# GPS graph layer: edge sums kept as 512 columns and a degree in a buffer of 750 nodes and projected once per chunk, with seven ring buffers in place of six

## The reference, cut to what matters

```python
# N = 6250 nodes of D = 256 columns, E = 106250 edges sorted by dst
xn = layernorm(x)
m = xn[src] @ W[:256] + edge_attr @ W[256:]              # one row for each edge
deg = segment_sum(ones, dst, 6250)
norm = where(deg > 0, rsqrt(max(deg, 1)), 0)
h = segment_sum(m * norm[dst][:, None], dst, 6250) + h_bias
x = x + h + mix(xn)      # mix: linear attention over all nodes, 8 heads, then a GELU MLP
x = x + ffn(layernorm(x))  # two of eight experts, chosen by the mean of all rows, then a layernorm
```

## Time and profile before

| | us |
|---|---|
| median of 3 runs | 1607.79 (1602.73 to 1609.69) |
| the profiled execution, its own time | 1606.56 |
| its span, first to last instruction | 1604.4 |
| busy in the span: PE / PEld / DVE / ACT / POOL | 1129.4 / 741.1 / 671.4 / 543.1 / 918.7 |
| moved by DMA | 294.98 MB, mean 184 GB/s |
| mean granted TensorE clock | 0.877 of full |

### The profile page before, as it was taken

One profiled execution on the slowest core, in us unless ns is written; L12 is line 12 of the kernel. 1 busy time (PEld: TensorE's weight loads), 2 busy tenths in 40 slices (PEclk: granted clock), 3 DMA queues, 4 the chain that ended last, 5 costly groups with the idle time before them and its releaser, 6 DMA issues.

```text
span 1604.4 us, 22019 instructions
## 1 busy us (share of the span) xinstructions
PE 1129.4 (70%) x6879; PEld 741.1 (46%) x6879; DVE 671.4 (42%) x1784; ACT 543.1 (34%) x1129; POOL 918.7 (57%) x974
## 2 busy tenths in 40 slices
PE   0166757665676775565677777776777749999997
PEld 0023323332332332233344344444444449999997
DVE  5633334343433443321323233233332446677675
ACT  4731111111111111101233333333333356767673
POOL 6166666666666666666666666666666103434342
PEclk9987888888878888777799898897999969999999
DMA  9976666666666666486687777878777341222221
GB/s 244 314 235 191 196 186 191 191 195 179 206 181 196 191 196 188 126 262 206 203 247 232 240 231 258 239 226 254 233 242 221 100 130 41 76 65 70 72 62 40
DMA packets 209233, 294.98 MB, mean 184 GB/s; under 512 B 20940, under 2 KB 180146, under 8 KB 207887
## 3 DMA queue, kind: packets, MB, share of 16 engines
q1 hardware_dynamic: 152899, 165.66, 34.8%
q0 software_dynamic: 39888, 108.97, 22.5%
q10 hardware_dynamic: 16350, 19.20, 3.6%
HBM read 261.75 MB, written 32.00 MB: 183 GB/s over the span
## 4 chain that ended last, share of the span: by engine, by line
PE 33%; another core or an unknown queue 29%; issue 13%; DVE 12%; ACT 5%; DVEq 4%; DMA 2%; SPq 2%; ACTq 0%; POOL 0%; POOLq 0%
PE bank L1137 9%; PE bank L1148 8%; DVEq L1316 3%; PE bank L913 3%; PE bank L978 3%; PE bank L927 2%; PE bank L1021 2%; PE bank L921 2%; DVE acc L1318 2%; DVE xc L1326 1%; DVE lnst L1330 1%; DVE st L1184 1%; PE bank L1009 1%; DVE s L1280 1%
## 5 line engine op out<-in xcount | busy, mean ns | idle before, releaser
L575 POOL DMA_INDIRECT ring<-xn_table,src_sb x807 | 785.0, 973 | 434.3 <-issue 221.3
L913 PE MATMUL bank<-ring,s 128*32 128x512 f32 x1662 | 284.1, 656 | 64.1 <-DVE s L1280 40.4
L1289 DVE TENSOR_TENSOR pair<-s 128x128 f32<-128x128 f32 x70 | 20.5, 293 | 472.0 <-remote 423.1
L921 PE MATMUL bank<-ident,fl 128*128 128x128 f32 x280 | 60.4, 353 | 198.2 <-ACT fl L641 152.2
L978 PE MATMUL bank<-wstage,xt 128*125 128x512 f32 x200 | 134.4, 809 | 67.3 <-ACT xt L641 38.8
L921 PEld LDWEIGHTS bank<-ident,fl 128*128 128x128 f32 x280 | 38.5, 174 | 273.5 <-ACT fl L641 185.9
L927 PE MATMUL bank<-fl_t,wg 128*128 128x128 f32 x1120 | 148.4, 288 | 22.7 <-ACT fl_t L641 12.5
L927 PEld LDWEIGHTS bank<-fl_t,wg 128*128 128x128 f32 x1120 | 137.5, 200 | 24.9 <-ACT fl_t L641 13.5
L1318 DVE TENSOR_TENSOR acc<-acc,bank 128x96 f32 x277 | 70.7, 255 | 156.7 <-issue 87.6
L913 PEld LDWEIGHTS bank<-ring,s 128*32 128x32 f32 x1662 | 42.4, 113 | 190.6 <-issue 143.2
L702 ACT ACTIVATE kvn<-xc 125x512 f32<-125x512 f32 x50 | 31.5, 631 | 275.1 <-DVE xc L1326 220.4
(11 more groups left out here) (201 smaller groups left out, 2021.7 us busy)
## 6 DMA issues: line engine op xcount, KB each, us to landing
ring<-edges SPq DMA_DIRECT2D x207, 512.0 KB
ring<-xn_table,src_sb POOLq DMA_INDIRECT x807
xnr<-xn_table SPq DMA_DIRECT2D x50, 125.0 KB
xnr<-xn_table SPq DMA_DIRECT2D x25, 250.0 KB
xch<-x SPq DMA_DIRECT2D x25, 250.0 KB
base_rows<-xch ACTq DMA_DIRECT2D x25, 250.0 KB
x_rows<-xch ACTq DMA_DIRECT2D x25, 250.0 KB
xt_cols<-xte ACTq DMA_DIRECT2D x25, 250.0 KB
```

Of the source, the lines that this page charges most:

```text
L575: pool.indirect_dma_start(out=to, out_offset=None, in_=rows, in_offset=bass.IndirectOffsetOnAxis(ap=index, axis=0),).then_inc(done, 16)
L913: mm = pe.matmul(ps_seg[t % 2][j * W:(j + 1) * W, :], lhsT=s32[:, t % 3, j * TS + i, :], rhs=ring[:, u, j, :], start=i == 0, stop=i == TS ...
L921: mm = pe.transpose(ps_t[:, c * P:(c + 1) * P], fl[:, c * P:(c + 1) * P], ident[:, :])
```

## The change

It sums all 512 columns and the degree, unprojected, into `acc` of 5 planes for 750 nodes (three chunks of 250, used in turn, with 32 columns of overlap that are added back to the front at every lap). Once a chunk's sums are complete, the degree's root and reciprocal and the scaling are made on whole columns, PE projects the chunk straight into rows, ACT keeps them in a resident tile `x2` and zeroes the chunk's columns. `x2` first holds the normalised x, from which the key and value tiles are now read. The rows are no longer written to HBM and fetched, and the ring has seven slots. The core of the diff, with cuts:

```diff
-RS = 6
-NPAD = N + W + 6
+RS = 7
+RC = 3
+RN = RC * CN
+PLANES = 2 * KC + 1
-    FIN.append(max(DONE[c] + 1, FIN[-1] + 1 if c else 0, FIRST + 1 - (-6 * c // 5)))
+    FIN.append(max(DONE[c] + 2, FIN[-1] + 1 if c else 0, FIRST + 1 - (-6 * c // 5)))
+EMPTIED = [sum(d + 1 <= g for d in DONE) for g in range(NG)]
...
+        x2 = sb("x2", [TN, NT, D])
-        acc = sbs("acc", [P, KC + 1, NPAD])
+        acc = sbs("acc", [P, PLANES, RN + W])
+        x_all = x2
...
-            def kv_load(n):
-                wait_past(sp, s_xt, n - 2 * XN + 1)
-                sp.dma_start(kv_tile(n), table[n * TN:(n + 1) * TN, :]).then_inc(s_xk[kv_slot(n)], 16)
...
-            def fetch(c):
-                rows = x2_d[c * CN:(c + 1) * CN, :].rearrange("(t p) d -> p t d", p=TN)
...
+            for e in sorted(set(EMPTIED)):
+                lo, hi = EMPTIED.index(e) * ST, min((NG - EMPTIED[::-1].index(e)) * ST, NS)
+                pool.memset(roof[0:1, lo:hi], float(CN * (e + RC) - W)).then_inc(s_roof, 1)
...
-            act.wait_ge(s_tab, TABLE_DONE)
-            for b in range(NB):
-                zero(b * BLK * D, (b + 1) * BLK * D).then_inc(s_zero, 1)
-            def evict_t(t):
-                act.wait_ge(s_tp, t + 1)
-                wait_past(act, s_pj, t)
-                copy(fl_t[:, :, :], ps_t[:, :].rearrange("p (c n) -> p c n", c=4)).then_inc(s_flt, 1)
+            def degree_roots(c):
+                act.wait_ge(s_nrm, 2 * c + 1)
+                nc.scalar.activation(nrm[:, :], nrm[:, :], ACT.Sqrt).then_inc(s_sqd, 1)
+            def park(c):
+                act.wait_ge(s_prj, c + 1)
+                act.wait_ge(s_xt, 2 * c + 2)
+                copy(x2[:, 2 * c:2 * c + 2, :], ps_f[0:TN, :].rearrange("p (t d) -> p t d", t=2)).then_inc(s_park, 1)
+            def refill(c):
+                act.wait_ge(s_prj, c + 1)
+                empty(ring_columns(c), ring_columns(c) + CN).then_inc(s_emp, 1)
-            def store_rows(n):
...
-                if i == 1 and 1 <= t <= NG:
-                    evict_t(t - 1)
+                if i == 0 and done_at(t, 1) is not None:
+                    degree_roots(done_at(t, 1))
+                if i == 0 and done_at(t, 2) is not None:
+                    park(done_at(t, 2))
+                    refill(done_at(t, 2))
...
             def transposes(t):
+                n = W * len(strips(t))
+                pe.wait_ge(s_cnt, t + 1)
+                wait_past(pe, s_acc, strips_before(t))
+                pe.matmul(ps_y[:, 0:n], lhsT=ones_r[:, :], rhs=counts[:, t % 2, 0:n], start=True, stop=True)
                 pe.wait_ge(s_fl, t + 1)
-                wait_past(pe, s_flt, t)
                 for c in range(4):
                     mm = pe.transpose(ps_t[:, c * P:(c + 1) * P], fl[:, c * P:(c + 1) * P], ident[:, :])
                 mm.then_inc(s_tp, 1)
-            def project(t):
-                projection().then_inc(s_pj, 1)
+            def project(c):
+                pe.wait_ge(s_scale, c + 1)
+                wait_past(pe, s_park, c)
+                for j in range(2):
+                    a = ring_columns(c) + j * TN
+                    for o in range(2 * KC):
+                        mm = pe.matmul(ps_f[0:TN, j * D:(j + 1) * D], lhsT=acc[:, o, a:a + TN], rhs=wg[:, o, :], start=o == 0, stop=o == 2 * KC - 1)
+                mm.then_inc(s_prj, 1)
...
-                pe.wait_ge(s_xk[kv_slot(n)], kv_rows(n))
-                    mm = pe.transpose(ps_xt[:, c * TN:(c + 1) * TN], kv_tile(n)[:, c * P:(c + 1) * P], ident[0:TN, 0:TN])
+                    mm = pe.transpose(ps_xt[:, c * TN:(c + 1) * TN], x_all[:, n, c * P:(c + 1) * P], ident[0:TN, 0:TN])
...
-                if i == 0 and 1 <= t <= NG:
+                if i == 1 and 1 <= t <= NG:
                     transposes(t - 1)
-                if i == 1 and t:
-                    columns_free(t)
-                    if fin_at(t, 0) is not None:
-                        node_columns(fin_at(t, 0))
-                if i == 1 and 1 <= t <= NG:
-                    project(t - 1)
+                if i == 2 and done_at(t, 1) is not None:
+                    project(done_at(t, 1))
...
             def sums(t):
-                v.wait_ge(s_pj, t + 1)
+                v.wait_ge(s_tp, t + 1)
+                wait_past(v, s_emp, EMPTIED[t])
                 for j in strips(t):
-                    v.tensor_tensor(acc[:, :, ds(b, W)], acc[:, :, ds(b, W)],
-                                    ps_y[:, 0:3 * P].rearrange("p (c n) -> p c n", c=3)[:, :, j * W:(j + 1) * W], ALU.add).then_inc(s_acc, 1)
+                    v.tensor_tensor(acc[:, :, ds(b, W)], acc[:, :, ds(b, W)], planes[:, :, j * W:(j + 1) * W], ALU.add).then_inc(s_acc, 1)
+            def spill(c):
+                v.tensor_tensor(acc[:, :, 0:W], acc[:, :, 0:W], acc[:, :, RN:RN + W], ALU.add).then_inc(s_spill, 1)
+                v.memset(acc[:, :, RN:RN + W], 0.0).then_inc(s_spill, 1)
+            def degrees(c):
+                v.tensor_scalar(nrm[:, :], acc[:, PLANES - 1, a:a + CN], 1.0, None, ALU.max).then_inc(s_nrm, 1)
+            def scale(c):
+                v.reciprocal(nrm[:, :], nrm[:, :]).then_inc(s_nrm, 1)
+                v.tensor_tensor(acc[:, 0:2 * KC, a:a + CN], acc[:, 0:2 * KC, a:a + CN],
+                                nrm[:, :].unsqueeze(1).broadcast_to([P, 2 * KC, CN]), ALU.mult).then_inc(s_scale, 1)
...
-                    x2_rows = v.scalar_tensor_tensor(xch[:, u, j, :], ps_f[0:TN, j * D:(j + 1) * D], norm[:, 2 * c + j:2 * c + j + 1], xch[:, u, j, :],
+                v.tensor_tensor(x2[:, 2 * c:2 * c + 2, :], x2[:, 2 * c:2 * c + 2, :], xch[:, u, :, :], ALU.add).then_inc(s_x2, 1)
```

More of the change, by code:

```diff
@@ L69 @@
 assert MIX[0] >= FOLD + 7 and all(m <= TS * g - 3 for m, g in zip(MIX, FIN)) and len(set(MIX)) == NC
+EMPTIED = [sum(d + 1 <= g for d in DONE) for g in range(NG)]
+assert len(set(DONE)) == NC
 MASKED = 1.0e6
@@ L283, in gps_layer @@
             "xl2", "xlb", "xb", "g2", "od", "rn", "res", "out"))
-        s_tl, TL = s_xk[0:2], [16 * len(range(u, NT, 2 * XN)) for u in range(2)]
+        s_tl = [sem(f"s_tl{u}") for u in range(2)]
         s_xfh, s_xfl, s_g1, s_gel, s_hh, s_hl, s_xs, s_vx, s_rx, s_bnx, s_rg = (sem(f"s_{n}") for n in (
@@ L463, in _ @@
                     edge_load(q)
-                if kv_at(q, 0) is not None:
-                    kv_load(kv_at(q, 0))
                 if q == FOLD:
@@ L515, in _ @@
                 sp.wait_ge(s_te[u], 16 * len(range(u, NC, 2)))
-            for c in range(2):
-                fetch(c)
             fetch_turned(1)
-            for c in range(2, AHEAD):
-                fetch(c)
             sp.wait_ge(s_top, 1)
@@ L922, in transposes @@
                 mm.then_inc(s_tp, 1)
-            def projection():
-                for o in range(KC):
-                    for c in range(4):
-                        mm = pe.matmul(ps_y[:, o * P:(o + 1) * P], lhsT=wg[:, c, o * P:(o + 1) * P], rhs=fl_t[:, c, :],
-                                       start=c == 0, stop=c == 3)
-                return mm
-            def project(t):
-                n = W * len(strips(t))
-                pe.wait_ge(s_cnt, t + 1)
-                pe.matmul(ps_y[:, KC * P:KC * P + n], lhsT=ones_r[:, :], rhs=counts[:, t % 2, 0:n], start=True, stop=True)
-                pe.wait_ge(s_flt, t + 1)
-                projection().then_inc(s_pj, 1)
+            def project(c):
+                pe.wait_ge(s_scale, c + 1)
+                wait_past(pe, s_park, c)
+                if c == 0:
+                    pe.wait_ge(s_par, 16 * 11)
+                for j in range(2):
[3 more added lines that the diff above has]
+                mm.then_inc(s_prj, 1)
             def fold_weights(step):
@@ L1109, in end @@
                 pe.wait_ge(s_pa, k * 2 + 2)
-                projection().then_inc(s_pp, 1)
+                for c in range(4):
+                    mm = pe.matmul(ps_f[0:TN, 0:D], lhsT=fl_t[:, c, 0:TN], rhs=wg[:, c, :], start=c == 0, stop=c == 3)
+                mm.then_inc(s_pp, 1)
             pe.sem_inc(s_gp, 1)
             def again(n):
-                if n == NC:
-                    pe.wait_ge(s_pv, 2 * PASSES + 1)
-                pe.wait_ge(s_xe, n)
-                node_columns(n)
                 turn_rows(n, NC)
```

226 lines of the change are left out of this document (99 added, 127 removed).

## The result

The changed kernel takes 1614.7 us (median of 8 runs, 1613.1 to 1618.7), the kernel before 1605.2 us in the same comparison (8 runs): a ratio of 1.0057, 95% interval 1.0044 to 1.0070. It is 0.6% slower, where 1543 us was forecast. The profiled execution has a span of 1611.3 us; that of before had 1604.4.

| us | before | after | difference | forecast |
|---|---|---|---|---|
| start to the first strip sums | 70.3 | 79.8 | +9.5 | +5 |
| first gather out of the table to the last | 1180.4 | 1164.3 | -16.1 | -75 |
| last gather to last sum | 24.5 | 25.4 | +0.9 | 0 |
| last sum to the mean of the rows | 10.0 | 20.6 | +10.6 | +6 |
| mean of the rows to the end | 316.5 | 318.5 | +2.0 | 0 |

What follows compares the result with a forecast made beforehand. The edge stage was taken as bound by POOL's gather pace plus 175 us of pauses for PE's late signals. Terms -88 - 5 + 18 + 5 + 6 = -64 from 1606.6 gave 1543 us; range 1456 to 1630.

Steps and rivals of the forecast that it cites:

- The loop, -88 us for half the pauses: Edge stage: seven slots and later transposes halve POOL's 175 us of waits, pause staying 2.6 us; bounds 0 and -175.
- Two groups for one pause: Edge stage: POOL gets two groups of twelve gathers done for each 2.6 us pause instead of one; part of -88 us.
- the pause grows with the run: Rival, edge stage: pause reaches 4.5 us after 24 gathers, loop gains only 23 us, total 1607 us; chance 0.12.
- slower: Rival, edge stage: one pause stays for each group, nothing gained in the loop, +24 us, 1630 us; chance 0.18.
- At 70% busy no wait of the rows is theirs: Edge stage DMA: 19 MB of 295 go, but no wait is due to that traffic, so no gain was counted.
- work costed at nothing: Edge stage: added DVE sums and reciprocal, ACT and PE work are hidden by idle time or POOL's pace; 0 us.
- DVE against POOL, +18 us: Edge stage: DVE's new scaling lengthens gathers beside it by 0.74 us for each of 25 chunks; bounds 0 and +34.
- The head, +5: Before the edge stage: eleven DVE instructions 4.7 us, four more raw tiles 2.3 us, less at most 1.8; bounds 0, +8.
- The end, +6: Last sum to router: reciprocal, scaling, projection and copy added, about 2.5 us of old steps gone; bounds +4 and +9.
- FFN, 0: FFN stage, 1288 us to the end: the change takes nothing from its products, so it stays at 317 us.

Runs made afterwards that it cites:

- free-running gathers: Edge-stage gathers go to a tile nobody reads, plain rows feed the sums, no edge loads, six slots: 2183 us; 1423 us on the faster chip.
- Two kernels: Changed kernel with `roof` memsets behind the eighth raw gather: ratio 1.0017; the same with six raw slots and no zeroing of the last chunk: 0.9969.
- half-column kernel: Changed kernel with each edge-stage gather fetching 128 columns in place of 256: ratio 0.9867 to the kernel before, on the faster chip.

## Why the prediction was wrong, point by point

- **The loop, -88 us for half the pauses.** This step failed. I saw that PE's signals are late and pass when POOL stops, and then priced the slots as if a longer run cost nothing but its gathers: half as many pauses, each of the same length. What ran was three pauses in ten fewer (87 to 60), each longer (2.03 to 2.39 us), because the gathers themselves hold PE back, as the free-running gathers show. What pauses have above the 0.30 us between any two gathers fell from 151 to 126 us in sum, and the gathers' lengthening rose by 14. With four fewer gathers, 5 us at 1.25, this is 16 us, as measured. (A reading was wrong there too: between 740.5 and 748 us DVE does work, from 743.06 on.) Over ten kernels with the ring as POOL's only wait, six or seven slots, early or late transposes, with or without scaling, edge loads or half the rows, the stage is 1.44 to 1.47 us per gather; the repeats of one and the same edge stage on three chips span 1.443 to 1.467, so what the loop's changes do inside that band is not resolved.
- **"Two groups for one pause".** True of five runs only; the mean run grew 1.4 times, almost without effect on the pace (1.463 to 1.450 us per gather). The rival "the pause grows with the run", which named a load that has to drain in any case, was the mechanism nearest to what ran; it got 0.12, and of "slower" the outcome is only just (0.57%). Its 4.5 us after twenty-four were 3.5, and its sum missed by the head and the end.
- **"At 70% busy no wait of the rows is theirs", DMA; work costed at nothing.** Right: without edge loads nothing changes. DVE's reciprocal (1.71 us a chunk, 42.8 in all) and PE's projection (108.8 us busy) do not show in the pace, nor do the 8 products per group that went; no run took them out one by one.
- **DVE against POOL, +18 us.** The lengthening was 14 us, 0.51 us for each of 28 gathers met, beside 0.74 us of common time: about two thirds, more than the 55% of the earlier trace rows. The Trainium skill ("SBUF — State Buffer", section "Who interferes with whom") has the other fully blocked; the profile shows neither that nor a cost in the total, since the version without scaling is no faster.
- **The head, +5.** The instructions were counted right and their surroundings not: POOL's later start (7.9 us) and four more raw gathers put the laps and a block's statistics under the gathers' hold. Two kernels gave back 2.4 and 7.1 of the 9.5 us in their profiles; that the hold is what makes the difference fits the faster chip's 70.2 to 73.0 us.
- **The end, +6.** Mis-sized, 10.6: the prices were right, 3.1 us of DVE's order were missed, and 0.5 us of ACT's zeroing and columns ahead of the last root.
- **FFN, 0.** It is 2.0 us longer; 1.2 of it one wait of the router on ACT (3.3 against 2.1 us). Not followed further.

## What to carry to other kernels

Before pricing a pause as slack, ask what it is for: whoever is waited for may be held back by the very work that the pause interrupts, and then fewer pauses come back as longer ones. Divide the stage by the resource whose count hardly changes: ten kernels show 1.44 to 1.47 us for a gather against an issue of 1.25, with six slots as with seven. A late signal has two readings, that its sender waited or that the sender is itself held up, and four matmuls without a wait between them that start 0.7, 1.4 and 2.1 us apart decide for the second. Taking the suspect away whole (plain loads for gathers: 300 us) says more than undoing the parts of a change one by one. It also points to fewer gathers, not more slots, as the next thing to try; that was not done here.

## What the runs showed of the hardware that I had not expected

- In five of six groups of runs, on at least four chips, indirect gathers issued by POOL without a break hold the other engines up, down to a tenth of PE's matmuls (236 against 2540 in 596 us, 102 against 481 us busy). The beat of 0.70 us is plainest where the hold is strongest. From 110 to 1150 us I took matmuls of one line that follow each other without a wait and start more than 0.9 us apart: with free-running gathers 84 of 89 such distances lie within 0.06 us of a multiple of 0.70 us, in the changed kernel 25 of 30, in the kernel before 8 of 19; with plain loads, with the wide memset behind each gather, and on the faster chip there is none. On one further chip nothing of this is seen and the kernel before takes 1483 us, 8% less. The stretch behind the mean of the rows, where nothing is gathered, takes the same on both kinds: 318.5 us in the changed kernel, 318.6 in the half-column kernel on the faster chip. Why the chips differ, and what the beat belongs to, stays open. The traces differ in another way too: for the same 19,880 instructions that of the half-column kernel on the faster chip holds 22,478 changes of semaphores, that of the changed kernel 8,071, and with plain loads on a chip of the first kind 22,066. Whether recording and holding up share a cause was not tried.
- A gather of 64 rows takes POOL 0.94 us in the mean, one of 128 rows 0.99, one with half the columns 0.99: an issue has nearly one price.
- Where the memsets of both rows (25 each) stand ahead of its first gather, POOL stood for 6.3 to 7.7 us before it, in all seventeen such profiles and on the faster chip too; for 0.2 us in the three kernels with only one row ahead. Why is open.
